# The passage between stages 1 and 2 of a four-stage network: first turned tiles in other banks and ahead of the last products, the tail of stage 1 behind the steps of stage 2

## Time and profile before

| | us |
|---|---|
| median of 3 runs | 1423.02 |
| lowest and highest | 1422.03, 1425.01 |
| the profiled execution | 1421.57 |
| its span in the trace | 1419.8 |
| PE busy in the span | 1349.5 |
| mean granted TensorE clock | 0.981 of full speed |

### The profile page before, as it was taken

One profiled execution on the slowest core, in us unless ns is written; L12 is line 12 of the kernel. 1 busy time (PEld: TensorE's weight loads), 2 busy tenths in 40 slices (PEclk: granted clock), 3 DMA queues, 4 the chain that ended last, 5 costly groups with the idle time before them and its releaser, 6 DMA issues.

```text
span 1419.8 us, 19459 instructions
## 1 busy us (share of the span) xinstructions
PE 1349.5 (95%) x7206; PEld 919.4 (65%) x7206; DVE 971.4 (68%) x1959; ACT 661.2 (47%) x1151; POOL 698.8 (49%) x836
## 2 busy tenths in 40 slices
PE   6988999999989999989999999999999999999998
PEld 5875445556455455554554437878888888888886
DVE  5997466665657766676746524677668767886787
ACT  6664233232323454445543574555444554454442
POOL 2676131421313323234332357588678768866864
PEclk9999999999998899999998999999999999999999
DMA  9100210103213021132120403422223232333210
GB/s 331 70 1 1 75 60 16 57 33 97 75 45 97 24 76 39 46 87 98 50 76 1 142 31 119 178 89 89 90 90 148 90 101 107 148 126 112 108 41 30
DMA packets 46270, 116.86 MB, mean 82 GB/s; under 512 B 3420, under 2 KB 4448, under 8 KB 42336
## 3 DMA queue, kind: packets, MB, share of 16 engines
q1 hardware_dynamic: 45104, 114.31, 23.9%
q10 hardware_dynamic: 1072, 1.31, 0.3%
HBM read 92.28 MB, written 23.07 MB: 81 GB/s over the span
## 4 chain that ended last, share of the span: by engine, by line
PE 67%; DVE 23%; ACT 5%; issue 3%; POOL 2%; DMA 0%; POOLq 0%; DVEq 0%; ACTq 0%
PE PS L1672 65%; DVE cm L630 5%; DVE SM L646 2%; DVE PS L833 2%; DVE SM L642 2%; PE PS L1681 1%; DVE tm L630 1%; DVE hm L639 1%; ACT EX L1257 1%; DVE hm L630 1%; DVE SM L647 1%; DVE SM L636 1%; DVE hd L639 1%; ACT ws_g L1078 1%; DVE qb L636 1%
## 5 line engine op out<-in xcount | busy, mean ns | idle before, releaser
L1257 ACT ACTIVATE EX<-PS 128x512 f32<-128x512 f32 (+3 forms) x384 | 170.1, 495 | 155.8 <-PE PS L1672 154.2
L1487 POOL TENSOR_TENSOR ws_g<-rw,ws_g 128x512 fp32r<-128x512 f32 x64 | 137.6, 2149 | 125.7 <-ACT ws_g L1078 125.7
L1487 POOL TENSOR_TENSOR SM<-SM 128x1 f32<-128x1 f32 x128 | 81.1, 634 | 226.9 <-DVE SM L636 224.2
L1672 PE MATMUL PS<-KG,QG 96*128 96x512 f32 (+3 forms) x384 | 141.6, 393 | 20.4 <-DVE SM L833 8.5
L1591 POOL TENSOR_SCALAR_AFFINE_SELECT EX<-EX 128x128 f32<-128x128 f32 x256 | 75.5, 303 | 162.7 <-ACT EX L1257 159.1
L833 DVE CUSTOM_DVE_ANT_0 PS<-PS,MW 128x128 f32<-128x128 f32 (+3 forms) x256 | 122.7, 500 | 46.8 <-PE PS L1672 46.2
L1672 PE MATMUL PS<-QG,KG 98*128 98x512 f32 (+3 forms) x384 | 135.6, 382 | 3.0 <-ACT EX L1257 2.8
L1456 ACT ACTIVATE ab<-hm 128x512 f32<-128x512 f32 x64 | 40.5, 633 | 204.6 <-DVE hm L630 204.6
L1672 PE MATMUL PS<-ws_d,HH 128*128 128x512 f32 x528 | 125.7, 389 | 0.3 <-DVE HH L630 0.3
L642 DVE TENSOR_REDUCE SM<-PS 128x1 f32<-128x512 f32 x128 | 87.8, 686 | 55.4 <-PE PS L1672 55.0
L1672 PEld LDWEIGHTS PS<-QG,KG 98*128 98x128 f32 x384 | 72.0, 193 | 76.4 <-issue 46.4
(11 more groups left out here) (204 smaller groups left out, 2799.7 us busy)
## 6 DMA issues: line engine op xcount, KB each, us to landing
rw<-in_L_ffn_w_gate SPq DMA_DIRECT2D x16, 1024.0 KB, 5.1
rw<-in_L_ffn_w_up SPq DMA_DIRECT2D x16, 1024.0 KB, 5.2
rw<-in_L_ffn_w_down SPq DMA_DIRECT2D x16, 1024.0 KB, 6.9
QG<-qs SPq DMA_DIRECT2D x48, 256.0 KB, 4.4
raw<-in_L_ffn_w SPq DMA_DIRECT2D x3, 2816.0 KB, 11.8
qs<-stg SPq DMA_DIRECT2D x16, 512.0 KB, 3.5
xA<-xs SPq DMA_DIRECT2D x2, 2048.0 KB, 9.1
ys<-xA SPq DMA_DIRECT2D x4, 1024.0 KB, 5.7
```

Source lines behind the costliest of these rows:

```text
L1257: e.activation(EX[:, n % 16, 0:W], PS[:, score_bank(n), 0:W], ACT.Exp, scale=ISQ, bias=0.0).then_inc(S["ex"], 1)
L1487: return e.tensor_tensor(out, a, b, op)
L1672: return e.matmul(out, l, r, start=start, stop=stop, skip_group_check=free)
```

## The change

- Banks: the first four of `misc` (turned tiles 0 to 3 of stage 2) take banks 0, 1, 4, 5. Banks 0 and 1 are free when the low parts xT1 of tiles 14 and 15 are made, banks 4 and 5 when DVE has read the products of tile 14.
- PE: `turn_x(0)` and `turn_x(1)` move into s = 19, between `quantized(10, 2)` and the last `project1`. Then follow turn_x(2), turn_x(3), quantized(11, 0), quantized(11, 1). quantized(11, 2) goes behind up2(0). up2 waits for pr and kv of 15 instead of 16.
- DVE: the loop of stage 1 ends after s = 18. Then: products1(14), the four low parts of turn_x, products1(15), the sums of 14 and 15, softmax1(6). The statistics of o0 for tiles 10 to 15 stand behind up2(n) for n = 0, 1, 3, 4, softmax1(7) behind up2(2). In every block, up2(n) now stands ahead of the mv3 statistics of that step.
- ACT: the loop ends after s = 19. keys1(15) and quantized(11, 0) stand behind the four high parts; quantized(11, 1) and the last exponential behind the sigmoid of n = 0, the norms1 of three pairs behind the sigmoids of n = 1, 2, 5. norm2 of tiles 4 to 7 writes xn2a, and waits no longer for x1 = 16.
- POOL: values1(13) ends stage 1; the statistics, values and sums of the last pairs are spread over n = 0 to 5.

```diff
@@ bank3 and freed
-            return (misc_no[t] + 4 if misc_no[t] < 2 else 6 + misc_no[t] % 2) if t in misc_no else top_no[t] % 3
+            if t in misc_no:
+                m = misc_no[t]
+                return (0, 1, 4, 5)[m] if m < 4 else 6 + m % 2
+            return top_no[t] % 3
...
-            if x < 2 and t in misc_no:
-                return "pr", NT - (x < 0)
+            if x < 4 and t in misc_no:
+                return ("xT1", NT - 1 + x + 2) if x < 0 else ("pr", NT - (x < 2))
@@ DVE
-            for s in range(21):
+            for s in range(19):
...
+            products1(14)
             for i in range(4):
                 turn_x(i)
+            products1(15)
+            scores1(14)
+            scores1(15)
             softmax1(6)
             for n in range(44):
                 k, j = divmod(n, 11)
+                up2(n)
                 if k < 3 and 3 <= j < 7:
                     i = 4 * (k + 1) + j - 3
                     w.wait_ge(S["x1"], i + 1)
                     stats(32 + i, xt(i), EPS, "mv3")
-                if n < 5:
-                    phase1(21 + n)
-                up2(n)
+
+                for i in {0: (10, 11), 1: (12, 13), 3: (14,), 4: (15,)}.get(n, ()):
+                    stats1(i)
+                if n == 2:
+                    softmax1(7)
@@ ACT
+                if i >= 8:
                     w.wait_ge(S["x1"], NT)
                     w.wait_ge(S["x2"], 4 * (i // 4 - 1))
-                norm(xn2[i >= 4][:, i % 4, :], xt(i), 32 + i).then_inc(S["xn2"], 1)
...
+                norm(xn2[i >= 8][:, i % 4, :], xt(i), 32 + i).then_inc(S["xn2"], 1)
...
-            for part in range(2):
-                quantized(11, part)
-            norms1(11)
+            keys1(15)
+            quantized(11, 0)
...
-                if n < 5:
-                    phase1(21 + n)
                 w.wait_ge(S["gt"], n + 1)
                 w.wait_ge(S["hd"], max(0, n - 1))
                 e.activation(sg2[:, n % 2, :], PS[:, 4, :], ACT.Sigmoid, scale=1.0 / XS, bias=0.0).then_inc(S["sg"], 1)
+
+                if n == 0:
+                    quantized(11, 1)
+                    exp1(7)
+                if n in (1, 2, 5):
+                    norms1({1: 11, 2: 13, 5: 15}[n])
@@ POOL
+            values1(13)
...
-                if n < 5:
-                    phase1(21 + n)
+
+                if n in (0, 1, 4):
+                    stats1({0: 11, 1: 13, 4: 15}[n])
+                if n == 2:
+                    values1(15)
+                if n in (1, 2, 5):
+                    rows1({1: 11, 2: 13, 5: 15}[n])
@@ PE
+            for s in range(20):
+                quantized(s - 9, 2)
+                if s == 19:
+
+                    turn_x(0)
+                    turn_x(1)
                 for k, i in stages(NT, 11, s):
                     if k == 4:
                         project1(i)
...
-                w.wait_ge(S["pr"], NT)
-                w.wait_ge(S["kv"], NT)
+
+                w.wait_ge(S["pr"], NT - 1)
+                w.wait_ge(S["kv"], NT - 1)
...
-            turn_x(0)
-            turn_x(1)
-            quantized(11, 0)
             turn_x(2)
             turn_x(3)
+            quantized(11, 0)
             quantized(11, 1)
-            quantized(11, 2)
             for n in range(44):
                 k, j = divmod(n, 11)
                 up2(n)
+                if n == 0:
+                    quantized(11, 2)
```

More of the change, by code:

```diff
@@ L690, in quantize, with products1 @@
                 ts1(below(c)[:, 0:n], raw[m][:, s:s + n], gone[m][:, 3:4], ALU.is_lt).then_inc(S["qm"], 1)
-            def scores1(i):
-                p, x = divmod(i, 2)
-                m = sm1[:, p % 2]
+            def products1(i):
                 w.wait_ge(S["kv"], i + 1)
@@ L700, in scores1 @@
                    k5[:, :, :, 0:1, :].broadcast_to([128, 2, 2, 8, 16]), ALU.mult).then_inc(S["pr"], 1)
+            def scores1(i):
+                p, x = divmod(i, 2)
+                m = sm1[:, p % 2]
                 w.wait_ge(S["pr"], i + 1)
@@ L713, in softmax1, with stats1 @@
                 tt(m[:, 3, :], m[:, 3, :], m[:, 2, :], ALU.mult).then_inc(S["at"], 1)
+            def stats1(i):
+                w.wait_ge(S["o0"], i + 1)
+                stats(16 + i, o0[:, i % 4, :], EPS, "mv2")
             def phase1(step):
@@ L721, in phase1 @@
                 if 5 in at_k:
+                    products1(at_k[5])
                     scores1(at_k[5])
-                if 7 in at_k and at_k[7] % 2 and step != 20:
+                if 7 in at_k and at_k[7] % 2:
                     softmax1(at_k[7] // 2)
                 if 8 in at_k and at_k[8] % 2:
-                    for i in (at_k[8] - 1, at_k[8]):
-                        w.wait_ge(S["o0"], i + 1)
-                        stats(16 + i, o0[:, i % 4, :], EPS, "mv2")
+                    stats1(at_k[8] - 1)
+                    stats1(at_k[8])
                 if 0 in at_k:
@@ L1120, in quantized, with keys1, exp1 @@
                     cp(o, pb[:, 0:n * 128].rearrange("p (c n) -> p c n", n=128)).then_inc(S["wq"], 1)
+            def keys1(i):
+                b = 4 + 2 * (i % 2)
+                w.wait_ge(S["kp"], i + 1)
+                w.wait_ge(S["o0"], max(0, i - 3))
+                cp(kvs[:, i % 4, :].rearrange("p (a n) -> p a n", a=2), PS[:, b:b + 2, 256:320]).then_inc(S["kv"], 1)
+            def exp1(p):
+                w.wait_ge(S["sd"], p + 1)
+                e.activation(sm1[:, p % 2, 2, :], sm1[:, p % 2, 1, :], ACT.Exp, scale=0.25, bias=0.0).then_inc(S["ex1"], 1)
             def phase1(step):
@@ L1124, in phase1 @@
                 if 5 in at_k:
[L1125 to L1129, removed]
+                    keys1(at_k[5])
                 if 3 in at_k:
@@ L1135, in phase1 @@
                 if 6 in at_k and at_k[6] % 2:
[L1136 to L1139, removed]
+                    exp1(at_k[6] // 2)
                 if step < 19:
@@ L1146, in phase1 @@
                     norm(xn1[:, i % 2, :], xt(i), i).then_inc(S["xn1"], 1)
-                if 9 in at_k and at_k[9] % 2 and step != 20:
+                if 9 in at_k and at_k[9] % 2:
                     norms1(at_k[9])
@@ L1162, in norm2 @@
                     w.wait_ge(S["tpm"], turned_no[("x", i - 4)] + 1)
+                if i >= 8:
                     w.wait_ge(S["x1"], NT)
                     w.wait_ge(S["x2"], 4 * (i // 4 - 1))
-                norm(xn2[i >= 4][:, i % 4, :], xt(i), 32 + i).then_inc(S["xn2"], 1)
-            for s in range(21):
+                norm(xn2[i >= 8][:, i % 4, :], xt(i), 32 + i).then_inc(S["xn2"], 1)
+            for s in range(20):
                 if 15 <= s < 19:
                     norm2(s - 15)
-                if s < 20:
-                    quantized(s - 9, 1)
+                quantized(s - 9, 1)
                 phase1(s)
@@ L1505, in pool_program @@
             w.wait_ge(S["ones"], 1)
-            def phase1(step):
-                for k, i in stages(NT, 11, step):
-                    if k == 10 and i % 2:
[L1511 to L1516, removed]
-                    if k == 7 and i % 2:
[L1518 to L1526, removed]
@@ new lines, in rows1, with stats1, values1 @@
+            def rows1(last):
+                for x in (last - 1, last):
+                    w.wait_ge(S["yn1"], x + 1)
+                    tt(xt(x), xt(x), yn1[:, x % 2, :], ALU.add).then_inc(S["x1"], 1)
+            def stats1(last):
+                for x in (last - 1, last):
+                    stats(16 + x, "mv2", "rs2", x)
+            def values1(last):
+                for x in (last - 1, last):
+                    w.wait_ge(S["at"], last // 2 + 1)
+                    w.wait_ge(S["yn1"], max(0, x - 3))
+                    k4 = kvs[:, x % 4, :].rearrange("p (g two d) -> p g two d", g=4, two=2)
+                    vb = k4[:, :, 1:2, :].broadcast_to([128, 4, 8, 16])
+                    ab = sm1[:, last // 2 % 2, 3, 32 * (x % 2):32 * (x % 2) + 32].rearrange(
+                        "p (g h d) -> p g h d", g=4, d=1).broadcast_to([128, 4, 8, 16])
+                    o = o0[:, x % 4, :].rearrange("p (g h d) -> p g h d", g=4, h=8)
+                    tt(o, ab, vb, ALU.mult).then_inc(S["o0"], 1)
@@ L1527, in phase1 @@
+            for s in range(20):
+                if 14 <= s < 18:
+                    stats(32 + s - 14, "mv3", "rs3", s - 14)
+                for k, i in stages(NT, 11, s):
+                    if k == 10 and i % 2:
+                        rows1(i)
+                    if k == 8 and i % 2 and s < 19:
+                        stats1(i)
+                    if k == 7 and i % 2:
+                        values1(i)
                     if k == 0:
                         stats(i, "mv1", "rs1", i)
[L1530 to L1533, removed]
+            values1(13)
@@ L1730, in project1, with bank_wait, turn_x @@
                 last.then_inc(S["kp"], 1)
-            for s in range(21):
-                if s < 20:
-                    quantized(s - 9, 2)
```

(13 more changed lines are left out.)

## The result

Over 20 executions each, the kernel before has a median of 1424.28 us (1418.73 to 1430.26) and the changed one 1419.94 us (1414.22 to 1426.56). The ratio is 0.9971, with a 95% interval of 0.9957 to 0.9985: 4.1 us faster, between 2.1 and 6.1. The first profiled execution of the changed kernel took 1417.55 us, with a span of 1415.8 us. (The 20 of the kernel before begin with the three shown ahead of the prediction, whose median was 1423.02.) 1419.94 lies in the forecast range and 1.9 above the point forecast of 1418.0; 1.3 of that is the higher median of the kernel before.

A forecast was written before the change was run, and what follows sets the result against it. PE was taken as the bound, busy 95% of the span with 67% of the last-ending chain. Terms 3.0 - 0.4 + 2.3 + 1.07 - 1.0 gave 5.0 us less, against 1423.02 a forecast of 1418.0 us, range 1416.0 to 1421.8.

The forecast's parts named there:

- the clock: PE around up2(0): granted clock stays full instead of falling, since PE pauses less; gain 2.3 us.
- norm2(4): ACT ahead of the n = 5 gate chain: norm2 no longer waits for x1, up2(5) starts earlier; gain 1.07 us.
- The four turns: Wait before up2(0): earlier turned tiles and DVE low parts start it at 118.05 instead of 121.03; gain 3.0 us.
- quantized(11, 2): PE: its six products leave the wait and stand between up2(0) and up2(1); loss 0.4 us.
- The table loads: ACT around sigmoid(1): moving the last exponential makes three loads instead of one, yet the sigmoid is early enough; nothing lost.
- Rival 2: ACT late at sigmoid(1) after two table switches and a copy, so gate chain 2 waits on PE; 1419.7 us, chance 0.05.
- mv3 in block 1: DVE in block 1: statistics behind up2 fall into a busy stretch, delaying copy CWT and PE; loss 1.0 us.
- rival 3: Attention's waits and clock drops eat the earlier start, so the total does not change; 1423 us, chance 0.15.

The follow-up runs named there:

- late_turns: Changed kernel with turn_x(0) and turn_x(1) back behind the last project1, banks and other orders kept; entry to up2(0) 7.92 us instead of 8.51.
- before_norm2: Kernel before with only norm2 of tiles 4 to 7 written to xn2a, without the wait for x1 = 16; n = 1 to 5 took 20.73 us instead of 21.79.
- before_filled: Kernel before plus 14 unread PE products, ten ahead of turn_x(2), four behind quantized(11, 1); up2(0) to n = 1 took 3.52 us instead of 5.78.
- high_first: Changed kernel with mv3 ahead of up2 in blocks 1 and 2, all four turns behind project1, up2(0)'s high-part products first; ratio to before 0.9959.
- dve_as_before: Changed kernel with DVE's old order ahead of the low parts, new banks and early turns kept; entry to up2(0) 11.73 us, single execution 1429.48 us.

## Why the prediction was right

It named 5.0 us less; from entry to attention the profiles show 5.1 (338.73 less 333.63, and 4.95 in the second pair), and the timed runs 4.1 with an interval that holds both. The mechanism was right in each of its terms; in two places, the clock and norm2(4), the reasons given were weaker than the result. Step by step:

- *The four turns*: 3.0 expected, 2.87 measured (11.38 to 8.51). Right in size and in its chain (ACT behind kp, DVE behind ACT). The two early turns cost 0.6, where I had 0.3: I set the delay of kp against the first high part at 114.64 in the kernel before, 4.99 after the entry, but in the new banks and with late turns it comes 4.75 after the entry and not 5.34. The early turns hid no time at all: from the entry to attention late_turns takes 0.6 less (333.07).
- *quantized(11, 2)*: 0.4 expected. The distance of the second chain of up2(0) to the next is 2.06 instead of 1.73, so 0.33.
- *The clock*: 2.3 expected; 5.78 to 3.80 with the 0.33 of quantized added back is 2.3. The share of busy time that I had estimated for the new passage, 72%, was too high; it is 61% (2.35 of 3.85), as the pause is 1.50 and not 1.1. That is no more than the 63% of the row which I had leaned on, and one row was thin ground; but the clock stayed full in all six profiles with the new order and banks (3.79 or 3.80 in the table), so it was not the luck of one execution. And the 2.3 are not a constant of the old kernel: 2.3, 2.2 and, in before_norm2, 0.6 (4.16 less the 3.52 of before_filled; 0.25 of it is idle time behind a late sigmoid). Their mean over executions is what the runs pay, and that may be why the median gained a little less than 5; the scatter in attention would hide it either way.
- *The table loads*: none expected on the path, none found. From the start of a load to the start of what follows takes 1.30 (122.31 to 123.61, 123.88 to 125.18), so the 1.75 was a safe bound, and of the 1.38 us of drain which the Trainium skill (ScalarE: Activation LUTs, "What ACT_TABLE_LOAD costs") adds to a switch, nothing shows: the exponential ends at 123.87 and the next load begins at 123.88. Rival 2 falls.
- *norm2(4)*: 1.07 expected, 1.07 measured (21.79 to 20.72), and 1.06 in the run that made this edit alone. Its sigmoid was late, as I said, but by more: sigmoid(4) starts at 141.53, 2.5 us behind the end of its chain and not 1.4. It has more cover than the one chain that I gave it, as down2(3) stands there too; it ends at 142.11, 0.2 ahead of the next gate chain. That this sufficed was close to luck, and in high_first, which arrives 1.35 us sooner, it did not.
- *mv3 in block 1*: 1.0 lost expected, 0.82 to 0.84 measured. DVE was in truth without a pause in that window; the size was off because CWT lost only 0.87, and about 0.05 of that was recovered later.
- *No change downstream* (rival 3): of the 5.4 us by which attention starts earlier in the first pair, 4.0 are left at the end. With a scatter of 439.7 to 444.5 in attention alone, one pair says nothing on this. Layer 4 scatters too, in steps: from its first Silu to the end it takes 530.1 to 530.6 us in eight profiles, 533.4 to 533.6 in three, and 536.6 in dve_as_before, and in the last four the long DVE operation shown there stands ahead of PE's extra idle time, once or twice. (In the first profiles of both kernels it stands at a third place, 470 us into the layer, and costs nothing.) Whether a part of the gain is lost in attention stays open.

## What to carry to other kernels

Where an engine's order is written by hand, look at the last wait before the bound engine starts, and put only what feeds it ahead of it; what nobody awaits goes behind the first long steps, but not ahead of anything that a later step awaits. A free bank and a free engine are both needed: of the 3.5 us that both brought (11.4 to 7.9), the new order without the banks brought 1.0, and the run with the banks but the old order on DVE brought nothing. And when a step arrives earlier, the next wait on its in-order neighbours has to be cut too: here a normalisation ahead of a sigmoid ate 0.85 of 1.35 us until the two changed places.

## What the runs showed of the hardware

The granted TensorE clock fell to half (1.2 GHz) after a stretch of thin PE work (1.64 us busy in the 3.85 before it), but not always at the same place of the same program: it fell at 118.9, 118.5 and 117.3 us in three profiles with the old passage (9.3, 9.0 and 8.6 after the entry), for 6.8, 6.8 and 3.4 us, and cost between 0.6 and 2.3. Useless products in the pause kept it at 2.4 GHz and were worth 1.9 us at the start of attention.

One and the same DVE operation on 1536 numbers in each partition took 2.55 us in one execution and 8.11 in another, with POOL's operations beside it slower in the first and faster in the second. Where it stood ahead of PE, it made the execution some 3 us longer, without any change of the clock.
